# Twelve 128-row tiles transposed by VectorE in 32 x 32 blocks and by DMA, in place of TensorE

## The reference

```python
qkv = jnp.einsum('bsc,cf->bsf', x, Wqkv) + bqkv
attn = softmax(jnp.einsum('bqd,bkd->bqk', q, k) * scale)
out = jnp.einsum('bqk,bkd->bqd', attn, v)
...
x = x + _layernorm(_L0_attn_ref(_layernorm(x), Wqkv, bqkv, Wo, bo))
x = x + _layernorm(_L0_ffn_ref(_layernorm(x), W_gate, W_up, W_down))
```

## Time and profile before

| | |
|---|---|
| runs (3) | 1677.01 us median, 1674.39 to 1677.29 |
| the profiled execution | 1675.49 us, its span 1673.6 us |
| PE busy | 1651.5 us, 99% of the span |
| VectorE busy | 1113.2 us, 67% |
| ScalarE busy | 636.6 us, 38% |
| GpSimd busy | 484.1 us, 29% |
| DMA queue | 161616 packets, 315.82 MB, 56.4% of 16 engines |
| granted clock | 0.999 |

### The profile page before, as it was taken

The page is one execution under the profiler, slowest core; times in us unless marked ns, Lnnn a source line. Parts: engine busy times, 40 slices in busy tenths (PEclk is TensorE's granted clock), DMA queues, the critical chain, the costliest instruction groups (busy, mean ns, idle before and its releaser), DMA issues.

```text
span 1673.6 us, 20937 instructions
## 1 busy us (share of the span) xinstructions
PE 1651.5 (99%) x7672; PEld 1373.1 (82%) x7672; DVE 1113.2 (67%) x1625; ACT 636.6 (38%) x1149; POOL 484.1 (29%) x409
## 2 busy tenths in 40 slices
PE   7999999999999999999999999999999999999998
PEld 6788888888878888888888888888888888888887
DVE  7975677877866666665556777855555555654676
ACT  3232444446533333333346644332232333344551
POOL 3431553554154545444211102511221111200003
PEclk9999999999999999999999999999999999999999
DMA  8461663567564545464579765844444454487772
GB/s 317 170 233 58 207 202 123 179 200 247 188 221 145 170 145 172 155 207 161 185 238 332 234 202 190 269 139 145 138 138 146 152 167 147 141 284 249 225 258 101
DMA packets 161716, 317.13 MB, mean 189 GB/s; under 512 B 13008, under 2 KB 41808, under 8 KB 158672
## 3 DMA queue, kind: packets, MB, share of 16 engines
q1 hardware_dynamic: 161616, 315.82, 56.4%
HBM read 212.21 MB, written 103.56 MB: 189 GB/s over the span
## 4 chain that ended last, share of the span: by engine, by line
PE 90%; DVE 6%; DMA 1%; issue 1%; ACT 1%; POOL 1%; DVEq 0%; SPq 0%; ACTq 0%; POOLq 0%
PE ps L343 27%; PE ps L345 27%; PE ps L344 27%; PE ps L1944 4%; PE ps L1840 3%; PE ps L1945 2%; PE ps L1889 1%; DVE norm_x_stats L1293 1%; DVE xt_f L1341 1%; DVE y_all L1760 1%; DMA tt<-wgt_dram 1%; DVE xn_t L1312 0%; PE ps L1890 0%; DVE slots L1312 0%; DVE xc L1312 0%
## 5 line engine op out<-in xcount | busy, mean ns | idle before, releaser
L1312 DVE TENSOR_TENSOR slots<-w_raw,slots 128x512 fp32r<-128x512 f32 x500 | 405.6, 833 | 266.6 <-ACT slots L1117 266.2
L1117 ACT CAST slots<-w_raw 128x512 fp32r<-128x512 f32 x504 | 302.1, 621 | 467.5 <-PE ps L345 458.3
L343 PE MATMUL ps<-xc,slots 128*128 128x512 f32 x1208 | 471.1, 390 | 1.8 <-DVE u L1636 1.7
L345 PE MATMUL ps<-xc,slots 128*128 128x512 f32 x1208 | 470.2, 389 | 0.0
L344 PE MATMUL ps<-xc,slots 128*128 128x512 f32 x1208 | 470.0, 389 | 0.0
L343 PEld LDWEIGHTS ps<-xc,slots 128*128 128x128 f32 x1208 | 226.8, 188 | 49.2 <-DVE u L1636 2.1
L345 PEld LDWEIGHTS ps<-xc,slots 128*128 128x128 f32 x1208 | 226.8, 188 | 47.1
L344 PEld LDWEIGHTS ps<-xc,slots 128*128 128x128 f32 x1208 | 226.8, 188 | 47.0
L345 PE MATMUL ps<-slots 128*128 128x512 f32 x572 | 222.6, 389 | 0.0
L343 PE MATMUL ps<-slots 128*128 128x512 f32 x572 | 222.6, 389 | 0.0
L344 PE MATMUL ps<-slots 128*128 128x512 f32 x572 | 222.5, 389 | 0.0
(11 more groups left out here) (189 smaller groups left out, 2389.5 us busy)
## 6 DMA issues: line engine op xcount, KB each, us to landing
w_raw<-hsp_dram SPq DMA_DIRECT2D x154, 256.0 KB, 3.9
hsp_dram<-hs SPq DMA_DIRECT2D x20, 1792.0 KB, 8.3
w_raw<-wffn SPq DMA_DIRECT2D x134, 256.0 KB, 3.7
w_raw<-wffn SPq DMA_DIRECT2D x56, 512.0 KB, 6.2
w_raw<-wdt_dram SPq DMA_DIRECT2D x88, 256.0 KB, 3.9
wgt_dram<-tt SPq DMA_DIRECT2D x21, 1024.0 KB, 8.3
w_raw<-wgt_dram SPq DMA_DIRECT2D x84, 256.0 KB, 2.8
xc_raw<-xq_dram SPq DMA_DIRECT2D x9, 1024.0 KB, 5.8
```

Of the source, the lines that this page charges most:

```text
L343: pe.matmul(dst, stat(HIGH), mov(HIGH), start=first, stop=False, skip_group_check=reread)
L345: return pe.matmul(dst, stat(LOW), mov(HIGH), start=False, stop=last, skip_group_check=reread)
L1117: act.copy(operand(n, HIGH), source(n)).then_inc(w_high, 1)
L1312: return dve.tensor_tensor(dst, src, high.bitcast(F32), ALU.subtract)
```

## The change

PE no longer transposes x1n of tiles 0 to 11, and ScalarE no longer copies them out. VectorE transposes x1n in blocks of 32 x 32 into a new tile `y_tile` (`x1_blocks`, one instruction). SP stores `y_tile` to `y_dram` (`store_blocks`) and, at the start of the next tile's turn, loads it into `xt_tile` with four DMAs, one for each 32 partitions, in runs of 32 numbers (128 bytes), which puts the blocks in their places (`load_blocks`). `store_xq` and `first_sums` then wait for `y_moved`. The late tiles 12 to 15 stay as they were, with renumbered semaphores.

```diff
+            def store_blocks(u):
+                sp.wait_ge(y_ready, u + 1)
+                sp.dma_start(y_dram[u], y_tile[:]).then_inc(y_stored, 16)
+
+            def load_blocks(u):
+                sp.wait_ge(y_stored, 16 * (u + 1))
+                if u > 1:
+                    sp.wait_ge(xq_stored, 32 * (u - 1))
+                if TPB <= u - 2 < 2 * TPB:
+                    sp.wait_ge(xs_done, 4 * (u - 2 - TPB) + 4)
+                for b in range(P // SQ):
+                    sp.dma_start(xt_tile[u % 2][b * SQ:(b + 1) * SQ, :, :].rearrange("j k (a i) -> j k a i", i=SQ),
+                                 y_dram[u].rearrange("(a j) (k b i) -> b j k a i", j=SQ, b=P // SQ, i=SQ)[b]
+                                 ).then_inc(y_moved, 16)
...
             for t in range(2, TILES):
+                if t >= 4:
+                    load_blocks(t - 4)
                 if t == TILES - 1:
                     sp.wait_ge(q_low, TILES)
                     load_xc(0, A11, 0, 0)
...
+                if 3 <= t < TILES - 1:
+                    store_blocks(t - 3)
                 store_x1(t - 2)
...
-                pool.wait_ge(xq_evicted, 2 * (TPB + i) + 2)
+                pool.wait_ge(y_moved, MOVES * 16 * (TPB + i + 1))
...
                 exponentials(t)
-                if t >= 4:
-                    evict_xq(t - 4, 0)
...
-                if t >= 4:
-                    evict_xq(t - 4, 1)
                 o_out(t - 1)
...
+            def x1_blocks(u):
+                dve.wait_ge(x1n_done, u + 1)
+                if u > 0:
+                    dve.wait_ge(y_stored, 16 * u)
+                dve.transpose(y_tile[:], x1n[:, u % 2, :]).then_inc(y_ready, 1)
...
                     a_moments(t - 2)
+                if 3 <= t < last:
+                    x1_blocks(t - 3)
                 o_out(t - 1)
...
-                if t >= 4:
-                    transpose_x1n(t - 4, 0)
                 for g in range(4):
...
-                    if t >= 4 and g == 2:
-                        transpose_x1n(t - 4, 1)
```

More of the change, by code:

```diff
@@ L163, in pair_k @@
     return KP - 1 if p == MIXED else (p - 1) // 2
+SQ = 32
+MOVES = P // SQ
 LATE_LOAD, LATE_STATS, LATE_NORM, LATE_MORE, LATE_STORE = 2, 3, 4, 5, 6
@@ L226, in transformer_block @@
     xt_tile = [at("xt_even", 188, [KC, P]), at("xt_odd", 148, [KC, P])]
+    y_tile = at("y_tile", 200, [C])
     xp_tile = at("xp_tile", 176, [2, KH, P])
@@ L261, in transformer_block @@
     hsp_dram = nc.dram_tensor("hsp_dram", [PASSES, PRODS, KP, P, BLOCK], F32)
+    y_dram = nc.dram_tensor("y_dram", [LNT, P, C], F32)
     stats_dram = nc.dram_tensor("stats_dram", [BLOCKS, 2, BLOCK], F32)
@@ L312, in transformer_block @@
     x1_stored, x1n_done = sem("x1_stored"), sem("x1n_done")
+    y_ready, y_stored, y_moved = sem("y_ready"), sem("y_stored"), sem("y_moved")
     xq_ready, xq_evicted, xq_stored = sem("xq_ready"), sem("xq_evicted"), sem("xq_stored")
@@ L533, in store_xq @@
             def store_xq(u, g, tile):
-                sp.wait_ge(xq_evicted, 2 * u + g + 1)
+                if u < LNT:
+                    sp.wait_ge(y_moved, MOVES * 16 * (u + 1))
+                else:
+                    sp.wait_ge(xq_evicted, 2 * (u - LNT) + g + 1)
                 if g == 0 and u > 0:
@@ L1078, in o_out, with evict_late @@
                 act.activation(o_half[:], ps[:, 6, D:2 * D], ACT.Copy, scale=inv_sum[:]).then_inc(o_halved, 1)
[L1080 to L1092, removed]
+            def evict_late(i, g):
+                act.wait_ge(xq_ready, 2 * i + g + 1)
+                act.copy(res[:, 1, cols(g, BLOCK)].rearrange("p (k t) -> p k t", k=KH),
+                         ps[:, late_bank(g), :].rearrange("p (k t) -> p k t", k=KH)).then_inc(xq_evicted, 1)
             def high(n):
@@ L1177, in _ @@
             act.wait_ge(x1_stored, 16 * (TILES - 3))
+            act.wait_ge(y_stored, 16 * LNT)
             for n in range(POOL_LOWS, SLOTS):
@@ L1247, in gates @@
                             if late_tile(p, stage) is not None:
-                                evict_xq(LNT + late_tile(p, stage), g)
+                                evict_late(late_tile(p, stage), g)
             def copy_out(P_, i, k):
@@ L1477, in a_out @@
                 if t >= TILES - 2:
-                    dve.wait_ge(xq_ready, 2 * (LNT - 2 + t - (TILES - 2)) + 2)
+                    dve.wait_ge(y_ready, LNT - 2 + t - (TILES - 2) + 1)
                 dve.wait_ge(a_ready, t * 2 + (h + 1))
@@ L1553, in x1_norm @@
                     if u > 1:
-                        dve.wait_ge(xq_ready, 2 * (u - 1))
+                        dve.wait_ge(y_ready, u - 1)
                     dve.wait_ge(norm_l.rstd_done, u + 1)
@@ L1948, in weigh @@
                     last.then_inc(pv_ready, 1)
-            def transpose_x1n(u, g):
-                if g == 0:
-                    pe.wait_ge(x1n_done, u + 1)
-                else:
-                    pe.wait_ge(xq_evicted, 2 * u + 1)
-                transposes(7, KH * g, x1n[:, u % 2, :], KH).then_inc(xq_ready, 1)
             def attend(t):
@@ L1965, in attend @@
                     if older and g == 0:
-                        if t > 4:
-                            pe.wait_ge(xq_evicted, 2 * (t - 4))
                         transpose_output(t - 2)
@@ L2021, in _ @@
                 transpose_probs(g, g)
-            pe.wait_ge(xq_evicted, 2 * LNT)
             transpose_output(last_tile - 1)
@@ L2058, in product @@
                             if P_ == 0 and late_tile(p - 2, stage) is not None:
-                                pe.wait_ge(xq_evicted, 2 * (LNT + late_tile(p - 2, stage)) + g + 1)
+                                pe.wait_ge(xq_evicted, 2 * late_tile(p - 2, stage) + g + 1)
                     if j == 3:
```

## The result

The changed kernel takes 1679.74 us (median of 16 runs, 1676.3 to 1683.24), the kernel before 1676.12 us beside it (16 runs, 1674.39 to 1677.5). The ratio is 1.0021, with a 95% interval of 1.0013 to 1.0028: slower by 3.6 us, a small difference, but its interval does not include no change. The forecast was 1676.8 us, "no change that can be measured"; it is missed by 2.9 us, and the time stands at the upper edge of the forecast's own range (1680). Among the chances, slower (0.42) and the same (0.40) had been nearly even. The profiled execution took 1677.81 us, 2.32 us more than before's 1675.49; its span is 2.4 us longer.

A forecast was written before the change was run, and what follows sets the result against it. PE, busy 99% of the span, was taken to bound the kernel, partly waiting for VectorE. -5.9 + 0.4 + 1.5 + 3.8 = -0.2 us gave 1676.8 us; own range 1673.5 to 1680, overall 1672 to 1689.

The forecast's parts named there:

- The tile's length and the removed transposes (-5.9): Attention loop: without x1n's transposes tiles 4 to 14 save 0.45 us each, tile 15 the full 0.93; -5.9 us.
- The first half: PE's first four x1n transposes per tile, claimed to fill time PE would otherwise wait for VectorE before `project_output`.
- VectorE's wait would not come back: Rival: PE would not wait for VectorE at `project_output`, so all 11.2 us count; 1671.5 us, chance 0.08.
- The block transposition (+0.4): VectorE ahead of `o_sum`: 1.2 us long, overhanging its room by 0.05 to 0.1 us in some ten tiles; +0.4 us.
- The packets: Block loads' 128-byte DMA packets: 17 ns each taken, 4.4 us of all 16 engines a tile; bounds 8.6 and 28.3 ns.
- The dear rival (28.3): Rival: each short DMA packet costs as much as one of 512 bytes, 28.3 ns; +9, 1686 us, chance 0.26.
- the cheap one (9): Rival: short DMA packets cost about 9 ns, nothing falls behind; -3.8, 1673.2 us, chance 0.14.
- The lag of SP's queue (+1.5): Tiles 9 to 12: DMA queue falls some 4 us behind, partly absorbed, delaying GpSimd's sums; +1.5 us, 0 with 13 ns.
- The end of attention (+3.8): Last four block loads, ahead of A11 in SP's queue, make it land 4.4 us later, stalling ScalarE and PE; +3.8 us.
- the slack of 0.6: End of attention: spare time before `o_half` and on PE, subtracted from A11's 4.4 us delay to give 3.8.
- the dear-packet bound: End of attention: the stall if each short packet took 28.3 ns, 6.8 us.
- The sign of the largest cost: Tile 15: ScalarE should wait some 4 us for A11, and PE with it; otherwise the largest cost is refuted.

The follow-up runs named there:

- the run without the round trip: The changed kernel with VectorE transposing straight into the tile stored as X, without y's store and the four block loads: 1669.12 us, ratio 0.9959 to before.
- `o_half` first: The changed kernel with ScalarE computing `o_half` of tile 14 ahead of the split of A11: 1678.88 us, ratio 1.0018 to before.
- split later: The changed kernel with ScalarE's split of A11 moved behind everything PE needs from ScalarE for tile 15: 1672.39 us, ratio 0.9978 to before.
- statistics later: As split later, with A11 loaded a turn earlier, VectorE's x1 statistics one score group later and x1n between the output projection's halves: 1671.25 us, ratio 0.997.
- direct stores alone: The changed kernel with eight stores per tile writing y straight into X, no block loads or X stores, tiles 4 to 7 read back: 1671.38 us, ratio 0.9973.

## Why the prediction was wrong, step by step

- **The tile's length and the removed transposes (-5.9).** Right: 16.36 us as read from tile 3, -4.87 us at tile 15, and for the 0.93 behind it the run without the round trip shows 0.89 (17.18 - 16.29). The first half was worth 0.02 us of its four transposes, as read. That VectorE's wait would not come back is refuted: it stands there twelve times with 0.2 us.
- **The block transposition (+0.4).** 1.19 us where I took 1.2, and 0 instead of +0.4: no wait for `o_sum` in the loop. The room was 0.1 to 0.35 us larger than its length.
- **The packets.** The block loads take 0.285 x 16 x 2000 / 707 = 12.9 ns each by the window 318 to 320 us, which holds nothing else (rows below). The straight line through the earlier trace rows said 13, and I had moved away from it to 17 on an argument that no row bore. The dear rival (28.3) is refuted, the cheap one (9) too. The Trainium skill's rule ("DMA: Bandwidth & Descriptors", "Why small descriptors are slow (HBM only)"), 10.4 ns by the estimate in the prediction, is nearer than my 17 and further off than the line. With it the sum would have been 3.2 us lower, not 1.7, since the text puts the lag of 1.5 at 0 from 13 ns down.

```profile
DMA packets 707, 0.09 MB, mean 44 GB/s; under 512 B 707, under 2 KB 707, under 8 KB 707
q1 hardware_dynamic: 707, 0.09, 28.5%
```

- **The lag of SP's queue (+1.5).** 0 in the profiled run, as the text said for 13 ns. But the engines are full there (share 0.97 and 1.02 from 349 to 382 us), and in `o_half` first, split later and statistics later VectorE waits for y's store in tiles 13 and 14. In the changed kernel's own profiled run it does not. I had priced the lag for GpSimd's sums and not for the single `y_tile`.
- **The end of attention (+3.8).** This is the step that failed, in the words "A11 lands later by the loads' own time, 4.4 us". With the measured 12.9 ns that would even be 3.4. Against a loop that is 4.87 us ahead A11 came 7.4 us late: the x1 store ahead of it came at 391.85 instead of 395.25 and so gained only 3.40 of the 4.87 us (1.5 lost); from there to the end of the weight stores it took 3.21 us instead of 1.80 (1.4 lost), since the two took 2.6 us to issue instead of 1.3; the four block loads held the queue for 6.8; and A11 landed 5.43 us behind its issue instead of 7.68 (-2.25). Less the slack of 0.6 that is 6.8, and the stall is 6.76, where 3.8 was predicted. That the dear-packet bound was also 6.8 is chance: the packets are not dear. The loads' own time, 3.4 us, is less than half of the 7.4. SP's queue before, ahead of the rows:

```profile
395.25 0.33 SPq L508 DMA_DIRECT2D x_dram<-x_even  x1
395.62 0.43 SPq L527 DMA_DIRECT2D wgt_dram<-tt  x1
```

- **The clock.** It stands nowhere in the prediction. It costs 2.48 us and, with the size of the stall, turns "no change" into "slower". It is as much as the whole growth of the span, 2.4 us.
- **The sum.** Predicted: -5.9 + 0.4 + 1.5 + 3.8 = -0.2. Profiled: -5.8 + 6.8 + 2.5 - 1.0 = +2.5, or 2.4 with the unrounded terms. The 1.9 us for two costs that did not come, and the 1.0 us at `u`, hid a part of the 5.4 us that were missing at the end, so it is luck that the time stayed within the range. Neither sign that was to make the prediction wrong came (a packet above 20 ns, a transposition above 1.6 us). The sign of the largest cost did, twice as large: ScalarE waited 8.22 us for A11 instead of some 4.

What stays open: why the time of the changed kernel spreads over 7 us and that of before over 3. The wait for y's store, 0, 0, 1.3 and 2.6 us in four profiled runs whose order is the same up to tile 15, would do it, but the timed runs have no trace. The 1.0 us at `u` is open too.

## What to carry to other kernels

When work moves from the bounding engine to the DMA engines, ask what is issued behind the new transfers in the same queue, and which in-order engine waits for it: here a split that nobody needed yet held up everything that PE needed at once, and moving it made a slower kernel faster than before. Mend the wait by lightening the transfer, not only by reordering: in the runs with full DMA engines each further cure moved the wait to another place. And price an idle time of TensorE of several microseconds at more than its length.

## What the runs showed of the hardware

- A block transposition of 128x1024 float32 on VectorE takes 1.19 us, or 1.16 ns for each element of a partition; its twelve rows in the changed kernel lie between 1185 and 1191 ns (row below). The Trainium skill ("VectorE: DVE Perf Modes", "The three transpose paths") warns that it transposes 32x32 blocks only and leaves their places, which is why the round trip is there.

```profile
L1578 DVE STREAM_TRANSPOSE y_tile<-x1n x12: 1185/1186/1191, 205.5 to 384.5; 128x1024 f32<-128x1024 f32 x12
```

- PE at half clock is as busy as at full (4.00 of 4.00 us). The stretch took 5.3 us in the changed kernel (410.23 to 415.56); the granted clock of 0.50 came behind each of six idle times of 3.5 to 7.8 us, one in each of six runs.
- A block load of 1024 packets takes SP between 0.61 and 2.64 us to issue (48 of them). The four ahead of A11 take 1.7 us on average (DMA share 0.92 from 395 to 403 us), and A11 is issued only behind them.
- Writing 128-byte pieces to DRAM is about as dear as reading them, an estimate from whole-run shares: direct stores alone keep the engines busy for 58.0% of 1668.2 us, the kernel without the round trip for 56.4% of 1667.0, 27.4 us less. In place of twelve stores of X it has twelve times 4224 packets of short writes and four tiles read back. With 1056 packets at the 28.3 ns of the earlier trace rows for each such store or readback, the short writes take (27.4 + 8 x 1.87) x 16 / 50688 = 13.4 ns each, against 12.9 for the reads; the rounding of the shares is worth 0.5 ns.
